# Unread products on TensorE in three of its waits

## The reference

```python
x = x + 0.5 * ffn(layernorm(x))
x = x + attn(layernorm(x))
x = x + 0.5 * ffn(layernorm(x))

def ffn(x):       # 128 -> 512 -> 128, ternary weights
    h = gelu(layer_norm(x, g1, b1) @ tern(w1).T + bias1)
    return layer_norm(h, g2, b2) @ tern(w2).T + bias2

def attn(x):      # 16 heads of 8 columns, 512 positions, 4 batches
    content = (q + u) @ k.T
    pos = relative_shift((q + v) @ (sinusoid @ Wp + bp).T)
    w = softmax((content + pos) / sqrt(8))
    return (w @ v) @ Wo + bo
```

## Time and profile before

| | before |
|---|---|
| median of three runs | 437.73 us (437.10 to 438.21) |
| the profiled execution, its time | 437.5 us |
| the profiled execution, its span | 435.7 us |
| busy: PE, PE weight loads | 352.1, 289.2 us |
| busy: DVE, ACT, POOL | 391.7, 264.1, 179.6 us |
| mean granted clock of TensorE | 0.969 |

### The profile page before, as it was taken

One profiled execution on the slowest core, in us unless ns is written; L12 is line 12 of the kernel. 1 busy time (PEld: TensorE's weight loads), 2 busy tenths in 40 slices (PEclk: granted clock), 3 DMA queues, 4 the chain that ended last, 5 costly groups with the idle time before them and its releaser, 6 DMA issues.

```text
span 435.7 us, 18133 instructions
## 1 busy us (share of the span) xinstructions
PE 352.1 (81%) x7344; PEld 289.2 (66%) x7344; DVE 391.7 (90%) x563; ACT 264.1 (61%) x642; POOL 179.6 (41%) x218
## 2 busy tenths in 40 slices
PE   1887798685979889798897988978889788964993
PEld 1665665563868668686686866867768677931683
DVE  8879888359999999999999999999999999919595
ACT  1687364336666666666666666666666666703990
POOL 7445747448322505325053250532505325024562
PEclk9999899989999999999999999999999999986798
DMA  7005257574121322213222132131322440200002
GB/s 218 1 2 173 70 157 225 134 206 111 37 79 26 87 66 46 77 26 82 63 41 78 21 86 64 39 79 27 80 63 39 85 75 14 68 3 2 0 26 72
DMA packets 58853, 31.01 MB, mean 71 GB/s; under 512 B 35470, under 2 KB 57454, under 8 KB 58702
## 3 DMA queue, kind: packets, MB, share of 16 engines
q1 hardware_dynamic: 57470, 29.18, 26.0%
q0 software_dynamic: 672, 0.49, 0.7%
q10 hardware_dynamic: 672, 0.80, 0.6%
HBM read 19.44 MB, written 10.88 MB: 70 GB/s over the span
## 4 chain that ended last, share of the span: by engine, by line
DVE 57%; issue 20%; PE 9%; ACT 5%; POOL 4%; DMA 2%; SPq 1%; DVEq 1%; POOLq 0%; ACTq 0%
DVE pT L981 28%; DVE negmax L967 20%; PE pair L1082 2%; DVE xh L788 2%; PE pair L1040 1%; ACT v_rep L671 1%; DVE sqsum L900 1%; ACT v_rep L683 1%; DVE x L914 1%; DMA qs_scratch<-pT 1%; POOL grs L519 1%; DVE stat L778 1%; DVE pT L948 1%; ACT pT L653 1%; PE pair L1063 1%
## 5 line engine op out<-in xcount | busy, mean ns | idle before, releaser
L719 ACT ACTIVATE probs<-pair,negmax 128x512 f32<-128x512 f32 x256 | 173.9, 684 | 103.6 <-DVE negmax L967 103.6
L981 DVE STREAM_TRANSPOSE pT<-probs 128x1024 f32<-128x1024 f32 x128 | 156.8, 1225 | 0.4 <-ACT probs L719 0.4
L967 DVE TENSOR_REDUCE negmax<-pair 128x2 f32<-128x1024 f32 x128 | 151.8, 1186 | 5.4 <-PE pair L1201 5.4
L1184 PE MATMUL pair<-stage_k,stage_c 128*32 128x512 f16 x1024 | 114.4, 395 | 33.9 <-ACT probs L719 30.9
L582 POOL TENSOR_TENSOR xh<-rowsum,xh 128x16 f32<-128x16 f32 x16 | 46.5, 2904 | 172.9 <-ACT probs L719 172.9
L1190 PE MATMUL pair<-stage_z,stage_q 128*32 128x512 f16 x1024 | 111.2, 381 | 0.0
L1201 PE MATMUL pair<-stage_z,stage_q 128*32 128x446 f16 (+58 forms) x1024 | 101.5, 280 | 0.0
L1196 PE MATMUL pair<-stage_z,stage_q 128*32 128x488 f16 (+55 forms) x1024 | 98.2, 275 | 0.0
L1225 PE MATMUL pair<-pT,v_diag 128*32 128x128 f32 (+1 forms) x2176 | 91.0, 270 | 0.0
L1184 PEld LDWEIGHTS pair<-stage_k,stage_c 128*32 128x32 f16 x1024 | 51.2, 140 | 47.7 <-ACT probs L719 37.3
L1225 PEld LDWEIGHTS pair<-pT,v_diag 128*32 128x32 f32 x2176 | 70.1, 113 | 2.0 <-issue 0.2
(11 more groups left out here) (116 smaller groups left out, 368.0 us busy)
## 6 DMA issues: line engine op xcount, KB each, us to landing
stage_z<-z_scratch SPq DMA_DIRECT2D x16, 254.0 KB
stage_q<-qs_scratch SPq DMA_DIRECT2D x116, 24.0 KB
qs_scratch<-pT SPq DMA_DIRECT2D x9, 256.0 KB, 2.6
stage_z<-z_scratch SPq DMA_DIRECT2D x16, 128.0 KB
kc_scratch<-pT SPq DMA_DIRECT2D x8, 256.0 KB, 4.1
stage_z<-z_scratch SPq DMA_DIRECT2D x16, 127.5 KB
stage_c<-qc_scratch SPq DMA_DIRECT2D x61, 32.0 KB
stage_k<-kc_scratch SPq DMA_DIRECT2D x15, 128.0 KB
```

The source lines that it names most:

```text
L719: nc.scalar.activation(probs[:, q % 6, :], score_pair(q // 2)[:, q % 2, :], ACT.Exp, bias=negmax[:, q % 8:q % 8 + 1], accum_out=rowsum[:, ...
L967: nc.vector.tensor_reduce(negmax[:, 2 * n % 8:2 * n % 8 + 2], score_pair(n)[:, :, :], AX.X, ALU.max, negate=True).then_inc(max_ready, 1)
L981: nc.vector.transpose(pT[:, par, 2 * n:2 * n + 2, :].rearrange("p a s -> p (a s)"), probs[:, 2 * n % 6:2 * n % 6 + 2, :].rearrange("p a s ...
L1184: mm(bank[32 * j:32 * j + 32, :], all_rows[:, 32 * j:32 * j + 32], stage_k[:, par, :], start=True, stop=False, skip_group_check=True)
```

## The change

PE gets three blocks of products that nobody reads. `fill(bank, count)` multiplies the fp16 weights `w1T` by themselves, 128 columns as the stationary and 512 as the moving operand, `count` times, into a PSUM bank that is overwritten afterwards with `start=True`. The blocks are of 10, 13 and 8 products; they wait for nothing and signal nothing. The first stands ahead of the wait for head 0's staged data, the second behind the last product of the attention, the third between the transposes of batch 0 and batch 1.

```diff
+IDLE_FIRST, IDLE_ADD, IDLE_TURN = 10, 13, 8
...
+            def fill(bank, count):
+
+                for _ in range(count):
+                    mm(ps[bank], w1T[:, 0:128], w1T[:, :], start=True, stop=True)
+
...
+            fill(6, IDLE_FIRST)
             pe.wait_ge(staged_pool, 16 * LOADS_POOL)
             head(0, 0, 16 * LOADS_EVEN, True)
...
             for b in range(B):
                 direct(H - 1, b).then_inc(wo_mm, 1)
+            fill(1, IDLE_ADD)
             for t in range(4):
                 ln_turn(2, t)
+            fill(1, IDLE_TURN)
             for t in range(4):
                 ln_turn(2, 4 + t)
             ffn(1)
```

## The result

| | before | after |
|---|---|---|
| median | 437.42 us (6 runs, 436.67 to 438.68) | 434.23 us (6 runs, 433.07 to 434.80) |
| ratio to before, 95% interval | | 0.9933 (0.9907 to 0.9958) |
| profiled execution: its time, span | 437.5, 435.7 us | 434.12, 432.3 us |
| mean granted clock of TensorE | 0.969 | 0.982 |

The change made the kernel faster: 0.9933 of 437.42 us is 2.9 us less, with an interval from 1.8 to 4.1. In a second series, with more runs, the same kernel came to 0.9968 (0.9952 to 0.9983), 1.4 us less.

What follows compares the result with a forecast made beforehand. The prediction took DVE to end the chain for 57% of the span, with PE's slow clock delaying others at a few places; 437.5 - 1.23 + 0.45 - 0.8 gave 435.9 us, range 434.0 to 437.4.

Steps and rivals of the forecast that it cites:

- the first rival: End of the attention: the 0.8 us shift keeps the clock there too, another 1.7 us won, 434.2 us; chance 0.2.
- the forecast's own band: Whole kernel: 435.3 to 436.4 us, with head 1's gap and the fall in `ffn(1)` at either end; chance 0.42.
- First block, 1.23 us: Ahead of head 0: ten hidden products keep the clock, so DVE's first maximum comes 1.23 us earlier.
- Tail, 0.8 us: Start of the second feed-forward: second and third block keep the clock; first gelu 0.8 us earlier, lower bound 0.46.
- the first transposes' earlier end: Start of the second feed-forward: four transposes end with their tiles, so ACT and POOL steps come some 0.15 us earlier.
- the two products: Before the first gelu: two products take 0.60 us instead of 1.06 until ACT can start, 0.46 us won.
- The three transposes: Start of the second feed-forward, before the hidden products: about 0.55 us instead of 0.79, counted as 0.25 us won.
- A fall inside `ffn(1)`, up to 0.4 us: Second feed-forward: PE's long pauses may lose the clock again, costing up to 0.4 us, counted in the range.
- The gap before head 1, +0.45 us as a consequence of the shift: PE's 3.02 us idle time before head 1, now earlier, loses the clock; first pair slower, 0.45 us lost, 0 if kept.
- the shift: From head 0 on, work comes 1.23 us earlier; 0.8 us of it is left at the end of head 15.
- End of the attention, 0, with 1.7 us as a rival: Last attention work: clock still falls, gain 0; if kept, 1.7 us more is won, chance 0.2.
- The rival by which the clock is rarely lost at 88 us, or trades places with the gap: Head 0: the first block is worth only 0 to 0.4 us, total 436.7 to 437.1 us; chance 0.22.

Runs made afterwards that it cites:

- the profile with five blocks: The change plus 11 products at the end of the attention and 12 in PE's idle time before head 1, against the kernel before: ratio 0.9919, 433.83 us.
- the run with four blocks: The change plus a block of 11 products at the end of the attention, ahead of the wait for `o_norm`, against the kernel before: ratio 0.9903, 433.30 us.
- the run with early blocks: The change plus 8 products at the attention's end and blocks of 30, 6 and 14 in the first feed-forward, against the kernel before: 0.9912, 433.17 us.

## Why the prediction was right, and where it wasn't

The forecast was 435.9 us, 1.6 under the profiled 437.5. Measured were 434.23, inside the range of 434.0 to 437.4 and near its lower end, and "faster" had most of the chance. That it lies inside is in part luck: 434.23 is outside the forecast's own band of 435.3 to 436.4, and the range reached so low only for the first rival, which did not come. Step by step:

- **First block, 1.23 us.** Measured 1.22 (2.87 to 1.65), in every profile. Right in place and size. The block was hidden in each of the eight profiles that have it, with 0.17 to 1.49 us of idle time left. From the end of DVE's L963 to the arrival it needs 2.46 us (2.63 - 0.17 in the profile with five blocks); the earlier trace rows leave 88.50 - 86.25 = 2.25, so with that timing it would have been some 0.2 us late, an estimate at the upper end of the prediction's 0 to 0.2.
- **Tail, 0.8 us.** Measured 0.71 to 0.72. Of the three terms two were right: the first transposes' earlier end 0.16 (0.15 predicted), the two products 0.46. The three transposes were sized wrong: they went from 0.79 to 396.85 - 396.16 = 0.69 us, 0.10 and not 0.25.
- **A fall inside `ffn(1)`, up to 0.4 us.** In the change the clock did not fall there, in spite of an idle time of 1.41 us at 400.4. In the run with four blocks it did, and cost nothing.
- **The gap before head 1, +0.45 us as a consequence of the shift.** This step failed. In both profiles of the change the clock was kept there. Of the seven kernels with the first block and none in the gap it was lost there, or as head 1 began, in four and kept in three; of the six without the first block it was lost in two, one of them the kernel before. So the shift doesn't decide, and neither does the place, as the prediction had it: the same gap of one kernel does both. Whether the shift changes the odds, 13 profiles can't tell. The price, read from how late PE came to head 14, depends on how much of head 1 the fall meets: 0.54 us where only the first pair was slow, as predicted; 0.88 to 1.04 where the second was slow too and DVE waited for each; 0.26 where the fall began behind the first pair (the run with early blocks).
- **End of the attention, 0, with 1.7 us as a rival.** The clock fell there in every profile of a kernel without a block at that place. The rival didn't come; its price is 1.55 us, a little under 1.7.
- **The time itself.** 1.22 + 0.71 = 1.93 us are the change's; 437.42 - 1.93 = 435.5, a ratio of 0.9956, which lies inside both intervals measured (0.9907 to 0.9958, and 0.9952 to 0.9983). The two profiles differ by 3.4 us, of which 1.41 are the arrival of head 0's data (88.50 against 87.09). I had taken the profiled 88.50 for the kernel's; of the 14 profiles it is the latest, and the others have 86.68 to 87.92 with and without the first block. 3.4 = 1.41 + 1.21 + 0.01 + 0.72 + 0.05. What the six runs of the kernel after had beyond 1.93 us is not settled: the second series did not repeat it.
- **The rival by which the clock is rarely lost at 88 us, or trades places with the gap.** At head 0 it isn't borne out: six of six profiles without the first block lost the clock. That the clock can differ between executions of one kernel came true at the gap.

## What to carry to other kernels

Unread products pay where PE is the one that others wait for just after its idle time, and only up to what PE's first work there takes too long at half clock; look in windows of 0.5 us, since in 40 slices a fall of 3.4 us shows only as an 8 among nines, which is easily passed over. Leave some of the gap free: with 11 products at the end of the attention 0.23 us were left, and one pause of 0.80 us for issue made PE late by 0.57; with 8 products 0.75 and 0.88 us were left and the clock was kept as well. And before a difference of two profiles is explained, divide both at events that the change can't touch: here that took 1.4 of 3.4 us away.

## What the runs showed of the hardware

- fp32 transposes by PE, put in place of the products, keep the clock at 2.4 GHz (1.00 in both windows above).
- The same idle time of 3.02 us at the same place kept the clock in one execution and lost it in another, of one and the same kernel.
- The granted clock in the records is not to be trusted at the very start: in the kernel before it stands at 1.00 up to 17 us, while L1063 takes 0.61 to 0.63 us there, as long as at 1.2 GHz in the earlier trace rows. In the run with early blocks, where PE worked from 0.99 us on, the same product takes 0.39 us at 14.07.

The last point rests on the timeline of PE and the window of the kernel before:

```profile
13.72 0.61 PE L1063 MATMUL pair<-v_rep,w1T 128*128 128x512 f16 x1 [0.47 <-ACT w1T L710]
...
12.00:15.00 3.00, 2.53 (x10) 1.62 (x11) 2.93 (x14) 0.80 (x2) 2.51 (x3) 1.00 0.00 0
```
